# Keys and lag transposes ahead of attention's output product, an eviction ahead of exponentials, and squares of two layer norms on ScalarE

## The reference

```python
def _layernorm(x, axis=-1, eps=1e-05):
    m = jnp.mean(x, axis=axis, keepdims=True)
    v = jnp.var(x, axis=axis, keepdims=True)
    return (x - m) / jnp.sqrt(v + eps)
...
x = x + _L0_xattn_ref(_layernorm(x), ctx_4096, ctx_4096)    # autocorrelation attention over 128 positions
x = x + _L0_ffn_ref(_layernorm(x), ...)                     # 1024x1024 linear + 8 experts of rank 16, top 2
x = x + _L1_xattn_ref(_layernorm(x), ctx_4096, ...)         # 128 channels, 8 heads, window of 16 columns
x = x + _L1_ffn_ref(_layernorm(x), ...)                     # 4 experts of rank 16, top 2
```

## Time and profile before

| | |
|---|---|
| median of 3 runs | 2117.87 us (2116.83 to 2118.1) |
| the profiled execution's own time | 2117.49 us |
| its span, first to last instruction | 2115.7 us |
| mean granted TensorE clock | 0.967 |
| PE busy | 1861.9 us (88%) |
| DVE busy | 1605.9 us (76%) |
| ACT busy | 1267.7 us (60%) |
| POOL busy | 1097.1 us (52%) |

### The profile page before, as it was taken

One profiled execution on the slowest core, in us unless ns is written; L12 is line 12 of the kernel. 1 busy time (PEld: TensorE's weight loads), 2 busy tenths in 40 slices (PEclk: granted clock), 3 DMA queues, 4 the chain that ended last, 5 costly groups with the idle time before them and its releaser, 6 DMA issues. The chain is left out here.

```text
span 2115.7 us, 49075 instructions
## 1 busy us (share of the span) xinstructions
PE 1861.9 (88%) x18912; PEld 1131.9 (54%) x18912; DVE 1605.9 (76%) x4622; ACT 1267.7 (60%) x1827; POOL 1097.1 (52%) x902
## 2 busy tenths in 40 slices
PE   5589899999899998989999989999898999998875
PEld 2355555555555555555555555555555555555543
DVE  3677788787888777788877788778778887778853
ACT  4266655666665566665566665566666556666542
POOL 2455554555555465555465555456555545555541
PEclk8899999999999999999999999999999999999985
DMA  5011111111110011110011111001111011111000
GB/s 207 13 38 51 50 37 36 36 40 50 50 50 30 30 50 40 50 50 30 32 47 40 50 50 50 30 30 40 50 50 50 32 36 41 40 50 40 20 1 21
DMA packets 24733, 91.56 MB, mean 43 GB/s; under 512 B 3136, under 2 KB 3264, under 8 KB 24576
## 3 DMA queue, kind: packets, MB, share of 16 engines
q1 hardware_dynamic: 24704, 91.17, 12.2%
HBM read 74.39 MB, written 16.78 MB: 43 GB/s over the span
## 5 line engine op out<-in xcount | busy, mean ns | idle before, releaser
L539 PE MATMUL pb<-w_base_h,even_words 128*128 128x512 f16 x1024 | 324.8, 379 | 0.4 <-ACT mid_t L831 0.4
L1318 POOL TENSOR_TENSOR p_hl<-sc,p_hl 128x512 f16<-128x512 f32 x128 | 177.6, 1387 | 181.7 <-ACT p_hl L720 181.7
L441 PE MATMUL pa<-ctx_a,tab 128*128 128x512 f32 x384 | 203.7, 656 | 34.5 <-ACT q_spec L720 23.3
L820 ACT ACTIVATE q_diag<-sc,par 32x1024 f32<-32x1024 f32 x192 | 215.9, 1141 | 19.9 <-DVE sc L1057 17.5
L441 PE MATMUL pa<-xn_a,tab 128*128 128x512 f32 x384 | 188.9, 615 | 44.0 <-ACT xn_a L720 43.4
L608 PEld LDWEIGHTS pc<-sc_t,v_diag 128*128 128x128 f16 x6144 | 171.3, 97 | 75.8 <-ACT rows_c L720 48.3
L608 PE MATMUL pc<-sc_t,v_diag 128*128 128x32 f16 x6144 | 174.2, 177 | 41.8 <-ACT rows_c L720 41.8
L1361 POOL TENSOR_TENSOR sc<-sc,sc_rec 128x512 f32<-128x512 f32 x128 | 133.9, 1046 | 147.2 <-DVE sc_rec L1133 147.2
L1311 POOL TENSOR_TENSOR rest<-rest,v_im 128x1024 f32<-128x1024 f32 x32 | 75.9, 2371 | 243.7 <-DVE v_im L1018 243.7
L720 ACT ACTIVATE rows_c<-pc 64x256 f32<-64x256 f32 x256 | 96.2, 376 | 165.5 <-PE pc L608 162.3
L539 PE MATMUL pb<-w_base_l,even_words 128*128 128x512 f16 x512 | 193.9, 379 | 0.0
(11 more groups left out here) (142 smaller groups left out, 4998.7 us busy)
## 6 DMA issues: line engine op xcount, KB each, us to landing
x_a<-in_x SPq DMA_DIRECT2D x32, 512.0 KB, 3.3
ctx_a<-in_ctx_in SPq DMA_DIRECT2D x32, 512.0 KB, 3.2
x_res<-in_x SPq DMA_DIRECT2D x32, 512.0 KB, 3.9
ctx_b<-in_ctx_in SPq DMA_DIRECT2D x32, 512.0 KB, 4.1
out<-rows_c SPq DMA_DIRECT2D x32, 512.0 KB, 2.9
v_diag<-in_base_w SPq DMA_DIRECT2D x1, 4096.0 KB, 14.4
tab<-in_spectra SPq DMA_DIRECT2D x1, 576.0 KB, 5.1
q_diag<-in_ra SPq DMA_DIRECT2D x1, 544.0 KB, 15.3
```

Of the source, the lines that this page charges most:

```text
L441: last = mm(place[:, n + h, :], lhsT, moving[:, h * HALF:(h + 1) * HALF], start=True, stop=True)
L539: mm(pb[:, h, :], rows[:, cols], weights[:, j, h * HALF:(h + 1) * HALF], start=(j == 0 and m == 0), stop=False)
L820: nc.scalar.activation(q_diag[rows, :, col:col + QB], source, ACT.Copy, scale=par[rows, a:a + 1]).then_inc(qd_out.sem, 1)
L1318: g_.tensor_tensor(part[:, :, :, LO], sc[:, g % 2, :, :], part[:, :, :, HI], ALU.subtract)\
```

## The change

Three edits, in one version:

1. TensorE's order: `b_keys` and `a_transpose` now stand ahead of `c_output`.
2. ScalarE's order: the eviction of the second group of attended products stands ahead of the first four exponentials; VectorE writes `neg_max` once for both halves (`a_lead`), and both calls of `a_exp` wait for it.
3. Layer norms 2 and 3: the two residual sums also write the sum of each row (`accum_out`). VectorE makes two one-column products of it: the sum times D to the power -1.5, the bias of a square on ScalarE, and the mean, D being 1024. The square is taken of (sum x D^-1.5 - x x D^-0.5), so that its accumulated row sum is the variance, which goes into `mv[n]`; its 1024 elements go into the buffer that `normalise` overwrites afterwards. On VectorE the residual sum into `rows_c` and its mean now stand behind `b_norm_rows` and `b_keys`.

```diff
--- before.py
+++ after.py
@@ -221,6 +221,8 @@
         rs_v = [little(1) for n in range(4)]
         rs_y = [little(1) for n in range(4)]
         rs_less = little(1)
+        ln_sum = [little(1) for n in range(4)]
+        ln_lead = [little(1) for n in range(4)]
         rs_shift = little(1)
         rs_power = little(1)
         rs_eps = little(1)
@@ -258,6 +260,8 @@
 
         ln_bn = [signal(f"ln_bn{n}", 2) for n in range(4)]
         ln_mv = [signal(f"ln_mv{n}") for n in range(4)]
+        ln_part = [signal(f"ln_part{n}") for n in range(4)]
+        ln_mean = [signal(f"ln_mean{n}") for n in range(4)]
         ln_eps = [signal(f"ln_eps{n}") for n in range(4)]
         ln_rs = [signal(f"ln_rs{n}") for n in range(4)]
         ln_less = signal("ln_less")
@@ -275,7 +279,7 @@
         mm_corr = signal("mm_corr", 2)
         top_found = signal("top_found", KT)
         top_gone = signal("top_gone", KT)
-        negmax_out = signal("negmax_out", 2)
+        negmax_out = signal("negmax_out")
         ninth_found = signal("ninth_found")
         ninth_gone = signal("ninth_gone", KT)
         exp_out = signal("exp_out", KT)
@@ -678,12 +682,13 @@
                     c_attend(c, 3)
                 if do_a:
                     a_context_long(i, 1)
+                if do_b:
+                    b_keys(b)
+                if do_a:
+                    a_transpose(i)
                 if do_c:
                     c_output(c)
-                if do_b:
-                    b_keys(b)
-                if do_a:
-                    a_transpose(i)
+                if do_a:
                     a_weights(i, 1)
                 if do_b:
                     b_values(b)
@@ -749,13 +754,23 @@
                     act.wait_ge(prod_q2.sem, prod_q2.after(b))
                 copy([v_re, v_im][n][:, :], pa_hi).then_inc(vagg_out.sem, 1)
 
+            def spread(b, n, rows, place):
+
+                act.wait_ge(ln_part[n].sem, ln_part[n].after(b))
+                if n == 2:
+                    act.wait_ge(tr_x[0].sem, tr_x[0].after(b))
+                else:
+                    act.wait_ge(pt_out.sem, pt_out.after(b))
+                nc.scalar.activation(place[:, :], rows[:, :], ACT.Square, bias=ln_lead[n][:, :], scale=-D ** -0.5,
+                                     accum_out=mv[n][:, 1:2]).then_inc(ln_mv[n].sem, 1)
+
             def a_query(b):
                 act.wait_ge(mm_q.sem, mm_q.after(b))
                 copy(q_spec[:, :], pa_hi).then_inc(q_out.sem, 1)
 
             def a_exp(b, h):
 
-                act.wait_ge(negmax_out.sem, negmax_out.after(b, h + 1))
+                act.wait_ge(negmax_out.sem, negmax_out.after(b))
                 for j in range(4 * h, 4 * h + 4):
                     nc.scalar.activation(prob[:, j, :], pa[:, h, (j % 4) * P:(j % 4 + 1) * P], ACT.Exp,
                                          bias=neg_max[:, j:j + 1]).then_inc(exp_out.sem, 1)
@@ -884,15 +899,18 @@
                     c_high(c, 2)
                     c_exp(c, 3)
                     c_high(c, 3)
+                if do_c:
+                    c_attended(c, 1)
                 if do_a:
                     a_exp(i, 0)
                 if do_c:
-                    c_attended(c, 1)
                     c_attended(c, 2)
                 if do_a:
                     a_exp(i, 1)
                 if do_c:
                     c_attended(c, 3)
+                if do_b:
+                    spread(b, 2, x_b, xn_b)
                 if do_a:
                     a_values_long(i, 1)
                 if do_b:
@@ -900,6 +918,8 @@
                 if do_a:
                     a_transposed(i, 0)
                     a_transposed(i, 1)
+                if do_c:
+                    spread(c, 3, rows_c, xn_c)
                 if do_b:
                     b_values(b)
                 if do_c:
@@ -959,7 +979,16 @@
                 dve_wait(dve, ln_bn[n], ln_bn[n].after(b))
                 v.bn_aggr(mv[n][:, :], bn[n][:, :, :]).then_inc(ln_mv[n].sem, 1)
 
+            def mean(b, n, rows_out):
+
+                dve.wait_ge(rows_out.sem, rows_out.after(b))
+                v.tensor_scalar(ln_lead[n][:, :], ln_sum[n][:, :], D ** -1.5, None, ALU.mult)\
+                    .then_inc(ln_part[n].sem, 1)
+                v.tensor_scalar(mv[n][:, 0:1], ln_sum[n][:, :], 1.0 / D, None, ALU.mult).then_inc(ln_mean[n].sem, 1)
+
             def normalise(b, n, rows, place):
+                if n in (2, 3):
+                    dve.wait_ge(ln_mean[n].sem, ln_mean[n].after(b))
                 dve.wait_ge(ln_rs[n].sem, ln_rs[n].after(b))
                 v.tensor_scalar(place[:, :], rows[:, :], mv[n][:, 0:1], rs_y[n][:, :],
                                 ALU.subtract, ALU.mult).then_inc(ln_out[n].sem, 1)
@@ -984,9 +1013,9 @@
                     v.match_replace(rest[:, j, :], top8[:, j, :], pa[:, h, (j % 4) * P:(j % 4 + 1) * P],
                                     GONE).then_inc(top_gone.sem, 1)
 
-                dve.wait_ge(top_gone.sem, top_gone.after(b, 4 * h + 4))
-                v.tensor_scalar(neg_max[:, 4 * h:4 * h + 4], top8[:, 4 * h:4 * h + 4, 0], -1.0, None,
-                                ALU.mult).then_inc(negmax_out.sem, 1)
+            def a_lead(b):
+                dve.wait_ge(top_gone.sem, top_gone.after(b))
+                v.tensor_scalar(neg_max[:, :], top8[:, :, 0], -1.0, None, ALU.mult).then_inc(negmax_out.sem, 1)
 
             def a_ninth(b):
 
@@ -1048,7 +1077,8 @@
                 dve.wait_ge(mm_ffn[0].sem, mm_ffn[0].after(b))
                 dve.wait_ge(bias_added.sem, bias_added.after(b))
                 v.scalar_tensor_tensor(out=x_b[:, :], in0=pb_all, scalar=1.0 / W_SCALE, in1=x_b[:, :],
-                                       op0=ALU.mult, op1=ALU.add).then_inc(x2_out.sem, 1)
+                                       op0=ALU.mult, op1=ALU.add, accum_out=ln_sum[2][:, :])\
+                    .then_inc(x2_out.sem, 1)
 
             v_halves = words(v_pad[:, :])
 
@@ -1144,11 +1174,8 @@
                 dve.wait_ge(mm_o.sem, mm_o.after(b))
                 dve.wait_ge(x2_moved.sem, x2_moved.after(b))
                 v.scalar_tensor_tensor(out=rows_c[:, :], in0=pc_all, scalar=bias_att[:, 3:4], in1=x_c[:, :],
-                                       op0=ALU.add, op1=ALU.add).then_inc(x3_out.sem, 1)
-
-            def c_norm(b):
-                dve.wait_ge(x3_out.sem, x3_out.after(b))
-                layer_norm(b, 3, rows_c)
+                                       op0=ALU.add, op1=ALU.add, accum_out=ln_sum[3][:, :])\
+                    .then_inc(x3_out.sem, 1)
 
             def c_norm_rows(b):
                 normalise(b, 3, rows_c, xn_c)
@@ -1200,6 +1227,7 @@
                 if do_a:
                     a_top(i, 0)
                     a_top(i, 1)
+                    a_lead(i)
                 if do_c:
                     c_transpose(c, 3)
                 if do_a:
@@ -1207,15 +1235,13 @@
                     a_softmax(i)
                 if do_b:
                     b_base(b)
-                    b_norm(b, 2, x2_out)
-                    variance(b, 2)
-                if do_c:
-                    c_attention_residual(c)
-                    c_norm(c)
-                    variance(c, 3)
+                    mean(b, 2, x2_out)
                 if do_b:
                     b_norm_rows(b, 2)
                     b_keys(b)
+                if do_c:
+                    c_attention_residual(c)
+                    mean(c, 3, x3_out)
                 if do_a:
                     a_products(i, 0)
                     a_products(i, 1)
```

More of the change, by code:

```diff
@@ L680, in step @@
                     a_context_long(i, 1)
-                if do_c:
-                    c_output(c)
                 if do_b:
@@ L686, in step @@
                     a_transpose(i)
+                if do_c:
+                    c_output(c)
+                if do_a:
                     a_weights(i, 1)
```

## The result

| | before | after |
|---|---|---|
| median, us | 2117.36 (4 runs, 2116.83 to 2118.1) | 2036.53 (4 runs, 2034.87 to 2038.82) |
| span of the profiled execution, us | 2115.7 | 2037.0 |
| ratio | | 0.9621, 95% interval 0.9607 to 0.9635 |

The time fell by 80.8 us, 3.8%. Forecast were 2045 us and 72.6 + 1 us of saving.

A forecast was written before the change was run, and what follows sets the result against it. TensorE was taken as the longest engine, yet idle 5.3 us of each 62.19 us step. Saving 1.20 + 1.38 less 0.16, so 2.42, in 30 steps plus 1 us took 2117.5 to 2045 us; range 2034 to 2084.

The forecast's parts named there:

- The eviction: TensorE's third group of attended products: the wait for ScalarE's evicted rows goes, 1.20 us a step.
- Keys and transposes ahead of the output: TensorE ahead of the weights: the output product covers the copies into xn_a, so the 1.38 us wait goes.
- What is late next: v_im: ScalarE's copy v_im, queued behind the second layer norm's square, delays TensorE's transposes; 0.16 us of 2.58 lost a step.
- VectorE's gain: Single neg_max on VectorE: one small multiplication less, making the sum into x_b 0.6 us earlier, or 0.1 at worst.
- Sum of a step: Saving per full step after the loss at v_im: 2.42 us, with 1.7 to 2.58 as ends.
- None of it matters for its own sake: Layer-norm work removed from VectorE saves nothing directly, since VectorE waits for TensorE at both places.
- The partial steps: First steps without attention and last two without first stage: together 1 us saved, range 0 to 2.5.
- The late v_im: Rival: the square keeps v_im late, leaving 1.4 us a step, 2075 us; chance 15 in 100.
- Only the 1.20: Rival: the weights wait equally long for something else, so only the eviction's saving stays, 2081 us; chance 12 in 100.
- the freed time comes back later: Rival: the saving is lost again later in the step, leaving 2117 us; chance 4 in 100.
- The table: Rival on ScalarE: square and exponential in different tables, two loads of 1.28 us a step, 2123 us; chance 6 in 100.

The follow-up runs named there:

- e1: Original kernel with only the second eviction of attended products moved ahead of the first four exponentials, neg_max left in two parts; 2078.95 us, ratio 0.9828.
- e4: Changed kernel with only layer norm 2 back on VectorE, layer norm 3 keeping its square on ScalarE; 2017.13 us, ratio 0.9536.
- e2: Original kernel with only TensorE's order changed, keys and transposes ahead of the output product; 2197.74 us, ratio 1.0390.
- e6: Changed kernel with layer norm 2 back on VectorE and neg_max written in two parts; 2038.98 us, ratio 0.9634.
- e3: Changed kernel with both layer norms back on VectorE, so without squares on ScalarE; 2048.51 us, ratio 0.9690.
- e5: Changed kernel with neg_max again written in two parts, both squares kept on ScalarE; 2051.70 us, ratio 0.9695.
- e7: Changed kernel with layer norm 2 on VectorE, plus one value-block copy of ScalarE moved behind q_spec and features into the next step; 2002.14 us, ratio 0.9463.
- e10: Changed kernel with layer norm 2 on VectorE, plus ScalarE evicting q_spec and features ahead of the values' copies; 2000.75 us, ratio 0.9450.
- e11: e10 with the second exponential and first high half of stage c also ahead of the values' copies; 1991.73 us, ratio 0.9414.
- e8: Changed kernel with the first square behind v_im in ScalarE's queue instead of ahead of it; 2039.20 us, ratio 0.9639.

## Why the prediction was right, and where its sizes were off

The forecast was 2045 us with a range of 2034 to 2084; 2036.53 lies within it, and 8 us below the forecast. By its steps:

- **The eviction.** Shown by e1: the wait goes and nothing takes its place. The term was mis-sized: 1.20 by the bracket, 1.38 measured.
- **Keys and transposes ahead of the output.** Shown by after: the wait for xn_a is gone. The term was 1.38 by the bracket; from the long transform to the weights it was 7.65, and it is 6.11 in e4, so 1.54, and from the weights to the values' product it was 1.82 and is 1.72, so 0.10 more. That it would not pay alone stood nowhere in the prediction. It took VectorE's new order, the residual sum of attention behind the low half of the keys, for granted as part of the change; e2 has that sum in its old place and is 80 us slower. I had priced that move at nothing, and it is a condition of the gain. The other parts are conditions too. Against e1 the step is 1.65 shorter in e4, but 1.25 with neg_max in two parts (e6) and 0.80 with the second square back on VectorE (e3).
- **What is late next: v_im.** The named mechanism is in the trace, with the size forecast in the bracket's measure (0.16 forecast, 0.17 in the row). The forecast was a difference of starts, though (43.0 against 42.84), and in starts the loss is 0.39. The links: square 1.15 forecast and 1.15 measured, read of the accumulator 0.1 and 0.19, VectorE's gain 0.6 and 0.66 to 0.68 (e5, e6). The overlap of 0.1 that I gave v_im with the read did not come: v_im starts 0.21 after the read's start. That and the longer read make v_im 0.1 later; the other 0.1 comes from the sum, which starts 0.09 behind the long transform where I had it 0.02 ahead.
- **Sum of a step.** 2.42 forecast, 2.62 measured. The measured parts are 1.38 + 1.54 + 0.10 - 0.39 = 2.63, the same within 0.01. Both waits were mis-sized low and the loss at v_im too, and part of this cancels.
- **"None of it matters for its own sake", said of VectorE's layer norms.** Wrong for the second: e3 less e4 shows 0.85 a step for it, as the wait of the transposes of stage c. For the first it was right that VectorE was idle there, and I did not follow it to its end: work put from an idle engine into a queue that is on the path could here only cost. e4 shows 0.41 a step for it.
- **The partial steps.** The forecast had 30 steps of 2.42 and 1 us for the partial ones. The 28 distances hold 28 of the 30: 73.4 measured, and 1.0 more in the long ones. The other two and the partial steps were forecast at 5.8 together; the last three distances gave 7.7 and the first residual sum took 3.4 back, 4.3 in all. The 5.1 between 73.6 forecast and 78.7 measured are thus 5.6 from the mis-sized step (28 x 0.20) and 1.0 from the long distances, less 1.5 that the first and last steps gave too little; that these partly cancel is luck.
- **The rivals.** The late v_im cost 0.39; its rival needed 1.18 (2.58 less 1.4). "Only the 1.20" is refuted by the 6.50, and "the freed time comes back later" by the steady distance. The table did not switch: the whole execution of after has one load, in the group view (busy us, mean ns, idle before).

```profile
L764 ACT ACTIVATE xn_b<-x_b,small 128x1024 f32<-128x1024 f32 x32 | 36.8, 1150 | 19.8 <-DVE small L985 19.8
L764 ACT ACTIVATE p_hl<-rows_c,small 128x1024 f32<-128x1024 f32 x32 | 36.8, 1149 | 80.0 <-DVE small L985 80.0
L764 ACT ACTIVATION_READ_ACCUMULATOR xn_b<-x_b,small 128x1 f32 x32 | 6.0, 188 | 0.0
L739 ACT ACT_TABLE_LOAD x1 | 1.3, 1283 | 10.3 <-POOL small L1315 10.3
```

With squares, exponentials, copies and identities between each other in 32 batches, these four share one table here. The Trainium skill (ScalarE: Activation LUTs, section Table sets: the hidden batching unit) gives the exponential's set 15 functions and names only some; its rule that functions of one set need no switch agrees with the trace, once the square is counted among them.

**Still open:** 0.10 of what the second part of neg_max costs in e6, the 1.7 us of the first steps, and what decides which of the equal steps is a long one.

## What to carry to other kernels

In a kernel of hand-ordered queues read the cost of a wait from starts, not from the bracket, and price an order on one engine together with the order that feeds it: TensorE's new order alone made the kernel 3.9% slower; together with VectorE's order and the single neg_max it was worth 0.8 us of each step, and 1.65 with the second square as well. Moving work off a busy engine helps only where that engine's next start is late: ask of each piece by itself whether its old place was a hole and whether its new place is one. Here one square of two was worth taking and the other not, and the two together hid it.

## What the runs showed of the hardware

- **Short waits can cost more than their length.** Seven of the 28 steps of after take 61.2 instead of 59.6 us. In one of them TensorE's first long transform, behind the wait for q_spec, takes 3.51; in a plain step it takes 1.98. The granted clock is 0.62 over 975 to 979 us, and 0.97 over the step (a plain step: 1.00):

```profile
975.65 3.51 PE L445 MATMUL pa<-ctx_a,tab 128*128 128x512 f32 x4 [0.78 <-ACT q_spec L725]
```

```profile
888.45:948.06 59.61, 56.68 (x592) 34.81 (x591) 46.73 (x142) 41.70 (x61) 33.48 (x28) 1.00 0.13 44
948.06:1009.31 61.25, 58.36 (x592) 35.46 (x591) 46.79 (x141) 41.81 (x61) 33.46 (x28) 0.97 0.12 43
975.00:979.00 4.00, 3.35 (x5) 1.18 (x6) 2.68 (x5) 3.95 (x7) 1.40 (x2) 0.62 0.00 0
```

  In the 58 us ahead of it the engine did just what it did ahead of a plain step's long transform, to within 0.1 us, with gaps of 0.78, 0.38 and 0.78 in the last twelve. In all seven long steps of after the clock falls at this place, 0.2 to 0.6 us behind the start of that product. Apart from e2, the runs that keep this gap have 3 to 9 long steps. In e7, e10 and e11, where it is gone, there are one, none and one, and in the two that are left the clock falls behind the other gap of 0.8, the one for mid_t, 2.1 to 2.2 us behind the start of that product. That a gap is a condition is thus likely; it was not tested by itself, and most steps have both gaps and stay at the upper level. In e2, with a gap of 3.1, 25 of 28 steps are longer.
- **The read of ScalarE's accumulator took 0.188 us**, a separate instruction behind each square. In after v_im starts 0.21 behind the read's start, in e8 k_h starts 0.09 behind it. VectorE's own read takes 0.083; the instruction behind the sum into x_b starts 1.23 after the sum with the read (after) and 1.22 without it (e4).
- **A small multiplication on VectorE took 0.72 or 0.17** for the same 4 columns: in the full steps the first of the two took 0.72 and the second 0.17. The one over 8 columns took 0.25. Why the first is longer no run shows.
